# Attention and MLP on one Trainium2 core: restack copies on two queues, scores in bursts of three from the MLP's third unit on

## The reference

```python
xn = layernorm(x)
# attention over each sequence of 256 tokens, 16 heads of 16 channels
q, k, v = split(xn @ Wqkv.T)
s = softmax(q k^T / 4) v                  # per head and sequence
s = s @ Wproj.T + bproj
# MLP, 256 -> 1024 -> 256
h = gelu(xn @ proj1.T + proj1_bias)
g = silu(h @ proj2.T + proj2_bias)
out = x + s * g
```

## Time and profile before

| | us |
|---|---|
| runs, median (lowest to highest of 3) | 142.09 (141.51 to 142.93) |
| the profiled execution, device time | 141.54 |
| its span | 139.7 |
| busy in it: TensorE / VectorE / ScalarE / GpSimd | 123.4 / 89.7 / 76.2 / 51.0 |
| mean granted clock of TensorE | 0.969 |
| DMA moved | 13.29 MB |

### The profile page before, as it was taken

How to read it: one execution, slowest core, us unless ns; L and a number is a source line. 1 busy time by engine, 2 the same in 40 slices (tenths; PEclk the granted TensorE clock), 3 DMA queues, 4 the chain that set the end, 5 groups by cost and what they waited for, 6 DMA issues and landing times.

```text
span 139.7 us, 2606 instructions
## 1 busy us (share of the span) xinstructions
PE 123.4 (88%) x980; PEld 93.3 (67%) x980; DVE 89.7 (64%) x178; ACT 76.2 (55%) x115; POOL 51.0 (36%) x53
## 2 busy tenths in 40 slices
PE   6569979999999899998899959998999999999530
PEld 5349768988899688785576736665677677676320
DVE  1558773300003999999999990589478666767563
ACT  3063348879971100114645679769768768875110
POOL 3268103999991000003355460199004002100610
PEclk9965899999999999999999999999999999999997
DMA  4899789999999999100000035000000101101102
GB/s 125 205 424 422 175 169 152 152 159 160 151 161 168 157 164 151 32 0 7 0 1 9 9 117 198 4 6 0 5 28 14 38 0 42 40 0 40 42 2 75
DMA packets 7553, 13.29 MB, mean 95 GB/s; under 512 B 1012, under 2 KB 2676, under 8 KB 7284
## 3 DMA queue, kind: packets, MB, share of 16 engines
q1 hardware_dynamic: 7108, 12.85, 42.7%
q10 hardware_dynamic: 432, 0.27, 1.4%
HBM read 5.51 MB, written 1.05 MB: 47 GB/s over the span
## 4 chain that ended last, share of the span: by engine, by line
PE 55%; DVE 28%; issue 6%; DMA 5%; ACT 4%; SPq 1%; DVEq 0%; ACTq 0%
PE bank L563 36%; DVE negm L480 21%; PE bank L679 11%; PE bank L651 7%; DMA wqkv_raw<-wqkv 5%; DVE yh L524 2%; DVE cd L497 1%; DVE fin L542 1%; ACT PT L404 1%; ACT cTh L420 1%; ACT xTh L351 1%; DVE gate L448 1%; PE bank L631 1%; SPq L235 1%; DVE rc L500 0%
## 5 line engine op out<-in xcount | busy, mean ns | idle before, releaser
L480 DVE TENSOR_REDUCE negm<-bank 128x4 f32<-128x1024 f32 x32 | 37.1, 1217 | 17.2 <-PE bank L631 17.2
L404 ACT ACTIVATE PT<-bank 128x1024 f32<-128x1024 f32 x32 | 31.0, 1022 | 7.0 <-PE bank L651 6.7
L316 POOL TENSOR_TENSOR hTl<-hG,hTh 128x512 fp32r<-128x512 f32 x16 | 20.4, 1303 | 30.9 <-ACT hTh L390 30.9
L679 PE MATMUL bank<-PT,VA 128*17 128x256 f32 x256 | 16.9, 382 | 0.0
L326 POOL TENSOR_TENSOR bg<-gate,bps 128x256 f32<-128x256 f32 x8 | 6.1, 760 | 29.0 <-DVE gate L448 29.0
L497 DVE STREAM_TRANSPOSE cd<-bank 128x256 f32<-128x256 f32 x16 | 7.2, 448 | 14.5 <-PE bank L679 14.5
L386 ACT ACTIVATE hG<-bank,b1s 128x512 f32<-128x512 f32 x16 | 11.0, 689 | 8.9 <-PE bank L563 8.8
L563 PE MATMUL bank<-w2h,hTh 128*128 128x256 f32 x64 | 15.2, 319 | 0.7 <-DVE yh L524 0.7
L414 ACT ACTIVATE th<-yh 128x256 f32<-128x256 f32 x8 | 3.3, 418 | 21.7 <-DVE yh L524 21.7
L563 PEld LDWEIGHTS bank<-w2h,hTh 128*128 128x128 f32 x64 | 9.6, 189 | 8.1 <-issue 7.2
L651 PE MATMUL bank<-qs,ks 50*128 50x256 f32 x128 | 12.8, 310 | 2.1 <-DVE negm L480 1.7
(11 more groups left out here) (72 smaller groups left out, 204.7 us busy)
## 6 DMA issues: line engine op xcount, KB each, us to landing
qs<-stage SPq DMA_DIRECT2D x12, 256.0 KB, 12.3
ks<-stage SPq DMA_DIRECT2D x12, 256.0 KB, 19.2
w_raw<-w SPq DMA_DIRECT2D x2, 1024.0 KB, 10.0
xs<-x SPq DMA_DIRECT2D x4, 256.0 KB, 6.0
xb<-x SPq DMA_DIRECT2D x1, 1024.0 KB, 5.0
out<-fin SPq DMA_DIRECT2D x8, 128.0 KB, 1.7
wqkv_raw<-wqkv SPq DMA_DIRECT2D x3, 256.0 KB, 6.9
wps<-wp SPq DMA_DIRECT2D x8, 32.0 KB, 8.5
```

The costliest lines, as they stand in the source:

```text
L316: nc.gpsimd.tensor_tensor(hTl[:, n % FC, :], hG[:, n % FC, :], hTh[:, n % FC, :].bitcast(f32), ALU.subtract).then_inc(h_lo, 1)
L404: nc.scalar.activation(PT[:, w % 4], scores_of(*s), ACT.Exp).then_inc(exp_done, 1)
L480: nc.vector.tensor_reduce(negm[:, j, :, :, s[1] % 2, b].rearrange("p q a -> p a q"), scores_of(*s), axis=AX.X, op=ALU.max, negate=True).th ...
L679: last = nc.tensor.matmul(bank_of(*s)[32 * m:32 * m + VW, 0:SQ], VA[:, 2 * b + kt, 4 * j + m, :], PT[:, w % 4, m % 2, kt, :], start=(kt == ...
```

## The change

1. `restack` is a helper now. SP issues the copies of blocks 0 and 2 of both halves (partitions 0 to 47), ScalarE those of blocks 1 and 3 (partitions 64 to 111): block 1 behind its copy of block 2, block 3 of half 0 between its copies for XT 2 and XT 3, block 3 of half 1 ahead of its first gelu.
2. The order: both V halves, then two F1, then S. The scores come in bursts of three (the last has two), with the other six F1 of half 0, the first 22 parts of F2 and the F1 of half 1 between them, by a weight (1.9 for an F1, 1 for a part). MT 2 moves into the output stage, MT 0 and 1 come two bursts behind their last score. In the output stage the remaining 10 F2 parts stand in slots 0 to 5, 8, 9, 12 and 13.
3. V is evacuated by VectorE instead of ScalarE.
4. ScalarE's high part of the projection weights moves from behind the fifth exponential to ahead of the gelu of F1 8.

```diff
+AHEAD = 6
+BURST = 3
+LEAD = 2
...
-    order += [("V", 0, p) for p in range(2)]
-    order += [("F1", n) for n in range(FC)]
-    order += [("V", 1, p) for p in range(2)]
-
-    gaps = [[("F2", n, 2 * part), ("F2", n, 2 * part + 1)] for n in range(TT // 2) for part in range(2)]
-    gaps += [[("F1", n)] for n in range(FC, 2 * FC)]
-    for n, gap in enumerate(gaps):
-        order += gap
-
-        order += [("S", 2 * n), ("S", 2 * n + 1)]
-        if n and PAIRS[n - 1][1] == B - 1:
-            order.append(("MT", PAIRS[n - 1][0]))
-    assert len(gaps) == len(PAIRS)
-    ffn = [("F2", n, part) for n in range(TT // 2, TT) for part in range(4)]
+    order += [("V", h, p) for h in range(2) for p in range(2)]
+    order += [("F1", n) for n in range(LEAD)]
+
+
+
+    ffn = [("F2", u, part) for u in range(TT) for part in range(4)]
+    filler = [(("F1", n), 1.9) for n in range(LEAD, FC)] + [(s, 1) for s in ffn[:2 * TT]]
+    filler += [(("F1", n), 1.9) for n in range(FC, 2 * FC)] + [(s, 1) for s in ffn[2 * TT:2 * TT + AHEAD]]
+    ffn = ffn[2 * TT + AHEAD:]
+    bursts = [range(n, min(n + BURST, 2 * len(PAIRS))) for n in range(0, 2 * len(PAIRS), BURST)]
+    share = sum(w for _, w in filler) / len(bursts)
+    at, turn = 0, [[], []]
+    for n, burst in enumerate(bursts):
+
+        order += [("MT", j) for j in turn.pop(0) if j < 2] + [("S", u) for u in burst]
+        turn.append([PAIRS[u // 2][0] for u in burst if u % 2 and PAIRS[u // 2][1] == B - 1])
+        while filler and at < (n + 1) * share - 0.5:
+            step, w = filler.pop(0)
+            order.append(step)
+            at += w
+    assert not filler
...
-        order.append(ffn.pop(0))
-        if g == 1:
-            order.append(("MT", HP // 2 - 1))
+
+        if j == 0 or b <= 1:
+            order.append(ffn.pop(0))
+        if g in (1, 2):
+            order.append(("MT", g + 1))
...
-                elif (kind in ring and s != ("MT", HP // 2 - 1)) or (kind == "F2" and s[1] < TT // 2):
+                elif (kind in ring and not (kind == "MT" and n > late)) or (kind == "F2" and s[1] < TT // 2):
...
+        def restack(queue, h, i):
+
+
+            cols = slice(h * HALF, (h + 1) * HALF)
+            stack, parts = (qs, (0, 0, 1)) if i < 2 else (ks, (0, 1, 0))
+            queue.wait_ge(qk_hi, 4 * h + i + 1)
+            queue.wait_ge(qk_lo, 4 * h + i + 1)
+            for n, part in enumerate(parts):
+                row = 64 * (i % 2) + n
+                queue.dma_start(stack[row:row + STK:3, :, cols].bitcast(f32),
+                                stage[:, h, i, part, :].bitcast(f32)).then_inc(stacked[h], 16)
+
...
+                for i in (0, 2):
+                    restack(sp, h, i)
...
+                    if b == 2:
+                        restack(act, 0, 3)
...
+                    if i == 2:
+                        restack(act, h, 1)
...
-                elif s[0] == "V":
-                    h, p = s[1:]
-                    act.wait_ge(v_made, n_v + 1)
-                    tt = 4 * h + 2 * p
-                    nc.scalar.activation(VA[:, tt:tt + 2, :, 0:HN],
-                                         bank_of(*s).rearrange("p (t n d) -> p t n d", t=2, d=HN),
-                                         ACT.Copy).then_inc(v_out, 1)
-                    n_v += 1
                 elif s[0] == "F1":
                     f = s[1] % FC
                     if n_f1 == 0:
+                        restack(act, 1, 3)
                         act.wait_ge(bias_in, 48)
                         act.wait_ge(xt_made, B)
                     if n_f1 == FC:
+                        act.wait_ge(wp_in, 128)
+                        act.wait_ge(stacked[1], 192)
+                        nc.scalar.activation(wph[:], wps[:], ACT.Copy).then_inc(wp_hi, 1)
                         act.wait_ge(f2_made, TT // 2)
...
+                elif s[0] == "V":
+                    h, p = s[1:]
+                    n_v += 1
+                    dve.wait_ge(v_made, n_v)
+                    tt = 4 * h + 2 * p
+                    nc.vector.tensor_copy(VA[:, tt:tt + 2, :, 0:HN],
+                                          bank_of(*s).rearrange("p (t n d) -> p t n d", t=2, d=HN)).then_inc(v_out, 1)
```

More of the change, by code:

```diff
@@ L62, in build_order @@
             order.append(("GATE",))
+    assert not ffn
     return order + [("PJ", 6, 0), ("PJ", 7, 0), ("PV", GROUPS - 1), ("TURN", 1, 3), ("PJ", 6, 1), ("PJ", 7, 1)]
@@ L182, in layer_kernel @@
         pj_made, gated, fin_done = sem("pj_made"), sem("gated"), sem("fin_done")
-        first_s = order.index(("S", 0))
+        first_s, late = order.index(("S", 0)), order.index(("F2", TT // 2, 0))
         ring = ("QK", "V", "F1", "MT")
@@ L344, in _ @@
             split_wqkv(1)
-            n_qk = n_v = n_f1 = n_mt = 0
+            n_qk = n_f1 = n_mt = 0
             for s in order:
@@ L404, in _ @@
                     nc.scalar.activation(PT[:, w % 4], scores_of(*s), ACT.Exp).then_inc(exp_done, 1)
-                    if w == 4:
-                        act.wait_ge(wp_in, 128)
-                        act.wait_ge(stacked[1], 192)
-                        nc.scalar.activation(wph[:], wps[:], ACT.Copy).then_inc(wp_hi, 1)
                 elif s[0] == "F2" and s[2] == 3:
@@ L455, in _ @@
             norm_apply(1)
-            n_qk = n_mt = 0
+            n_qk = n_mt = n_v = 0
             for s in order:
```

## The result

| | before | after |
|---|---|---|
| median us (lowest to highest), 4 runs each, same chip | 142.47 (141.51 to 142.93) | 146.22 (145.40 to 146.68) |
| profiled execution, device time / span | 141.54 / 139.7 | 146.68 / 144.6 |
| mean granted clock of TensorE in it | 0.969 | 0.944 |
| ratio after : before, 95% interval | | 1.027 (1.019 to 1.034) |

The change makes the kernel 2.7% slower. The forecast was 142.7 with a range of 139.1 to 145.7: wrong, and the median lies above the range. The two profiled executions differ by 5.1 us and the medians by 3.75, because the one of before is the second fastest and the one of after the slowest of theirs.

A forecast was written before the change was run, and what follows sets the result against it. TensorE was taken to bound the kernel everywhere, with VectorE's 32 reductions in the scoring stage. Issues +3.0, clock +1.7, waits -2.5, bursts -1.7, slots +0.5, F2 7.3 +0.7, tail -1.0 gave +0.7: 142.7 us, range 139.1 to 145.7.

The forecast's parts named there:

- the rate of the copies: Restack copies on two queues: 200 GB/s (bounds 151 and 300), first half landed at 36.5 plus a tail of 1 to 2.
- issues on ScalarE ahead of QK1.0: Six copy issues on ScalarE delay QK1.0 from 19.77 to about 22.8: +3.0 us (bounds +2.3 and +3.8).
- half level behind it: TensorE's clock falls to half after idling ahead of QK1.0: +1.7 us, the middle of 0 to 3.4.
- wait of S0 for the copies: At S0, reached at 38.55, the first half's copies have landed: no wait, 0; up to 4 at 151 GB/s.
- S0 to ST0: Scoring stage: 47.3 us of TensorE work plus 2.5 of waits, 49.8 in all, ST0 at 88.35.
- ST0 to the end of PV14: Output stage: 43.98 us less 3.6 for five F2 parts, plus 0.5 for slots; 40.9, PV14 ends at 129.25.
- tail behind PV14: After PV14, cTh follows the last exponential at once and PJ6 comes 2.4 us behind instead of 3.4: -1.0.
- the third rival: Copies to the two partition halves serialize at 151 to 160 GB/s, S0 waits 3 us: 145.7 us, slower; chance 0.20.
- Both waits on yh: Scoring stage: TensorE waits for yh behind VectorE's reductions, 1.3 us ahead of F1 9 and 1.2 ahead of F2 5.0.
- the 0.5 for the slots: Output stage: shorter PJ slots leave ScalarE's exponentials and tanh less cover, +0.5 us (bounds 0 and +2.5).
- Cheap issues, full clock: Rival: issues run beside ScalarE's copies at 0.5 us each, clock stays up; about 139.7 us, faster; chance 0.30.
- Slots bound by ScalarE: Rival: in the output stage ScalarE limits the slots, +2.5 instead of +0.5; 144.7 us, slower; chance 0.10.

The follow-up runs named there:

- e6: The changed kernel with SP issuing all copies except blocks 1 and 3 of half 0, which GpSimd's queue issues; 146.57 us in one run (before 141.29).
- e2: The kernel before with only the restack copies split over SP's and ScalarE's queues, at the change's places; 147.79 us, ratio 1.043.
- e3: The changed kernel with ScalarE issuing block 3 of half 0 behind its xTh copies of XT3 instead of ahead; 143.53 us, ratio 1.003.
- e1: The changed kernel with all 24 restack copies back in SP's queue, new order and V on VectorE kept; 148.02 us, ratio 1.042.
- e5: The changed kernel, all copies on SP, blocks 0 and 1, then 2 and 3, taken in turn; 144.81 us in one run (before 141.29).
- e7: The changed kernel, all copies on SP, eight F1 ahead of S0, four output-stage F2 parts done in the scoring stage instead of six; 144.49 us, ratio 1.021.
- e9: The changed kernel, all copies on SP, eight F1 ahead of S0, three output-stage F2 parts done in the scoring stage instead of six; 140.05 us, ratio 0.984.
- e11: The changed kernel, queues and all, with three F2 parts ahead of the output stage instead of six; 143.77 us, ratio 1.012.
- e10: The changed kernel, SP's copies alternating between partition halves, six F1 ahead of S0, three F2 parts ahead of the output stage; 137.90 us, ratio 0.974.
- e12: The kernel before with ScalarE issuing only blocks 1 and 3 of half 1, all of half 0 on SP; 151.08 us, ratio 1.058.

## Why the prediction was wrong

Two steps failed: the price of the issues on ScalarE (+3.0, measured +5.1), and the rate of the copies (200 GB/s and no wait, measured 164 GB/s and a last landing at 42.1). The first hid most of the second.

| step of the sum | forecast | measured | error |
|---|---|---|---|
| issues on ScalarE ahead of QK1.0 | +3.0 (22.8) | +5.1 (24.91) | +2.1 |
| half level behind it | +1.7 | +2.1 | +0.4 |
| V, F1 0, F1 1 up to S0 | | | +0.2 |
| wait of S0 for the copies | 0 | 0.9 | +0.9 |
| S0 to ST0 | 49.8 | 50.7 | +0.9 |
| ST0 to the end of PV14 | 40.9 | 41.1 | +0.2 |
| tail behind PV14 | -1.0 | -1.4 | -0.4 |
| net against the profiled execution of before | +0.7 | +4.9 | +4.2 |

**Issues on ScalarE: the mechanism was right, the size was not.** The place (ahead of the xTh copies of XT3), the order and the new wait on qk_lo were as forecast. The term was mis-sized by 2.1 us, and lay beyond its own upper bound of 3.8. I priced an issue at 0.70, from SP's second six in the earlier trace rows. Three issues took 2.84 and 2.82, 0.95 each in the mean (single ones 0.55 to 1.44). That is 1.5 of the 2.1. Another 0.3 is no cost of the issues: QK0.2's copy already stood at 17.16 instead of 16.82 in this execution. The bound, SP's first six at 0.96 each, had the right size by luck. Finer windows of before show 3.6 us for the first three of them and 2.08 for the next three, which were in SP's queue alone, so 0.69 each was a fair reading of that trace:

```profile
18.27 2.08 SPq L260 DMA_DIRECT2D qs<-stage  x3
```

What the trace of before could not show is two queues being filled at once. There SP's issues became slower too: its next three took 3.32 us in the changed kernel and 4.33 in e6, beside GpSimd's queue. Later in the changed kernel, behind 31, ScalarE's single issues took 0.55 again, and two together 1.30 and 1.28. e2 isolates the term (4.8 us), and e3 a part of it (3.3 us for the three issues and the earlier landing).

**The clock.** The half level lasted from 22.63 to 29.46; QK1.0 to V0.0 took 7.67 us instead of 5.59, 2.1 against the 1.7 forecast. The step was right, though its value was the middle of a range from 0 to 3.4.

**The rate of the copies: wrong, hidden by the first error.** Forecast 200 GB/s and a landing at 36.5 plus a tail of 1 to 2; measured 159 to 171 up to 40, and a last landing at 42.1. Had the first step been right, TensorE would have stood ready at about 38.7 and waited for a landing between 39.6 (e3) and 42.1: this error alone brings S0 one to three microseconds late. e1 shows it: ScalarE free, S0 at 41.2 after 6.17 us. So the third rival, that the halves serialize, described the stage well. It gave a wait of 3 us from 38.55 on and 145.7 us, the nearest of the forecasts to what came, and I gave it 0.20. I had argued from the swings of the rate that mixed halves are faster. In 24 to 40 the two queues were served about alike and wrote to different halves, and the rate was still 164. So mixing alone does not do it. But the other side isn't the rule either: the same two queues reached 252 at 42 to 48, and e3 225 and 245 at 32 to 40. Over all runs, windows of two to four microseconds with two queues range from 142 (e6) to 253 GB/s (e3), and what decides the rate is open.

The Trainium skill, "SBUF — State Buffer", in its section on hitting both halves with two DMAs, puts the gain at 6%. For 24 to 40 this trace agrees (164, 171, 162 and 159 GB/s, mean 164, against 157, 154, 167 and 155, mean 158: 4%). For 42 to 48 it doesn't (252 against 160, 58%), nor for one queue in turn in e5 (187 against 156, 20%, and 12% against e1). There the measurement decides: mixing can pay more than 6%, and can't be counted on to.

**The scoring stage.** 50.7 us against 49.8. Both waits on yh stood where they were forecast, at 1.3 (forecast 1.3) and 1.6 (forecast 1.2), and the remaining 0.5 lies spread over the work. TensorE's busy share was 94% (47.75 of 50.68), not above 95%. What I missed was not in the sum: that the unit which ends in this stage also holds the table load for the first exponential (e7 and e9), and that moving units out of it is worth some 2 us in the change (e11) and 5.3 where nothing else is late (e9 against e7, by the ratios).

**The output stage and the tail.** 41.1 against 40.9, but by two errors that cancel. From its true start at 82.92 this stage took 44.68 us before, not 43.98. Less the 3.6 for five F2 parts that is 41.1, as measured, so the 0.5 for the slots was not there. PJ6 came at 135.88, 2.0 us behind the end of PV14 instead of the 3.4 of the earlier trace rows (forecast 2.4):

```profile
135.88 0.36 PE L584 MATMUL bank<-wph,cTh 128*128 128x256 f32 x1 [0.99 <-DVE fin L563]
```

**The other rivals.** "Cheap issues, full clock" is refuted by QK1.0 at 24.91 and by e1. "Slots bound by ScalarE" is refuted by the output stage, which shrank by all of the 3.6 us.

**Whether the aim was worth it.** The prediction's limit for filling TensorE's idle time in the scoring stage was 5.0 us; with ST0 at 82.92 it is 39.4 less 35.1, or 4.3. No run went beyond it: e10 gets 3.9 of span. What the change needed was to put the right amount ahead of S0 (six F1 instead of two), to leave ScalarE alone, and to end no unit in the stage.

What stays open: why an issue takes 0.95 us at 17 to 24 and 0.55 to 0.65 behind 31. Both queues were being filled in the first stretch, and e6 shows the same on SP, but no run was made for it alone. Nor was it tried what sets the rate with two queues, which is also why the copies of half 0 landed at 42.1 in the changed kernel and at 39.6 in e3, where three of them were issued later; each was seen in the one profiled execution of its kernel. That the idle time causes the fall of the clock was not isolated: the mean clocks of e2 show it in some executions and not in others.

## What to carry to other kernels

Before moving a DMA issue to a compute engine's queue, price it above what a single queue shows (here 0.95 us instead of 0.69, while both queues were being filled), and look at what stands behind it on that engine: moving three issues by one step in the order gave back 3.3 us. Before pulling a consumer forward, find when its copies land, and ask what a second queue does to their order: one queue is also a priority. And look at what a unit of work that ends early leaves on the *other* engines, here a tanh between the reductions and a table load.

## What was not expected of the hardware

- The same issue on ScalarE took 0.95 us in the mean (six of them, 17.2 to 24.3) and 0.55 to 0.65 later (31.5 to 36.7). SP's three issues near 18.5 took 2.08 us alone (before), and 3.32 and 4.33 while a second queue was being filled (the change, e6).
- A second queue, filled with later transfers, delayed the last copy of the first from near 42 to 49.9 (e12). The total rate was unchanged up to 42 (160 GB/s), and 223 from there to 50.
- Strided copies to the two halves of the partitions, taken in turn in one queue, ran at 187 GB/s (one block after the other: 167 in e1, 156 before). In two queues they ran near 160 in some stretches and at up to 252 in others, with both queues served in both. e2 shows such a change from one stretch to the next:

```profile
28.00:32.00 4.00, 0.82 1.06 241
32.00:36.00 4.00, 1.00 1.09 162
```

- TensorE's clock fell to the half level within idle times of 5.5 us (the change) and 6.2 us (e1). In e7 it fell at 89.8, behind waits of 1.70 and 0.41 us, and stayed there for 6.8 us in which TensorE was busy throughout; in e11 it stayed for 10.2 us. An idle time of 1.70 us near the end of the kernel before was not followed by it until 138.
